# A kernel of two attention and two expert layers on one core: token rows for the first experts scattered to their slots during the first attention

## The reference, cut to what matters

```python
x = x + _L0_xattn_ref(_layernorm(x), ctx_512, ...)   # 16 heads of 8 over a context of 120 x 64
x = x + _L0_ffn_ref(_layernorm(x), Wr, br, W1, b1, W2, b2)   # 8 experts, each token goes to one
x = x + _L1_xattn_ref(_layernorm(x), ctx_512, ...)   # two attentions of 16 heads of 32, each with an MLP
x = x + _L1_ffn_ref(_layernorm(x), router_w, w1, w2) # 64 experts, top 4, capacity 128
```

## Time and profile before

| | us |
|---|---|
| median of three executions (2687.29 to 2694.06) | 2693.37 |
| the profiled execution | 2692.71 |
| its span, first to last instruction | 2691.0 |
| first attention, to the last scatter of token numbers | about 578 |
| first experts, to the last scatter of result rows | about 578 to 789 |
| second attention | about 789 to 2430 |
| second experts and final sum | about 2430 to 2691 |

### The profile page before, as it was taken

The page is one execution under the profiler, slowest core; times in us unless marked ns, Lnnn a source line. Parts: engine busy times, 40 slices in busy tenths (PEclk is TensorE's granted clock), DMA queues, the critical chain, the costliest instruction groups (busy, mean ns, idle before and its releaser), DMA issues. The chain is left out here.

```text
span 2691.0 us, 91904 instructions
## 1 busy us (share of the span) xinstructions
PE 2365.1 (88%) x33576; PEld 1821.1 (68%) x33576; DVE 2012.4 (75%) x6291; ACT 1605.7 (60%) x3346; POOL 1558.9 (58%) x2518
## 2 busy tenths in 40 slices
PE   6888888858768999999999999999999999975766
PEld 5666666647666777777777777777777777753544
DVE  4788888866454788888888888888888888754449
ACT  4556555624434777777777777777777777751110
POOL 1223333337753566666766676676667666646767
PEclk9999999979888999999999999999999999975555
DMA  6223111112110011100000000000000000001128
GB/s 138 65 65 104 50 41 43 42 29 52 42 36 5 7 40 40 38 8 9 9 6 9 8 8 6 8 8 8 7 8 9 8 6 8 5 5 32 48 89 264
DMA packets 129310, 95.31 MB, mean 35 GB/s; under 512 B 42367, under 2 KB 111697, under 8 KB 128482
## 3 DMA queue, kind: packets, MB, share of 16 engines
q1 hardware_dynamic: 109922, 72.53, 9.9%
q0 software_dynamic: 18944, 16.91, 2.4%
HBM read 51.59 MB, written 39.03 MB: 34 GB/s over the span
## 5 line engine op out<-in xcount | busy, mean ns | idle before, releaser
L1227 POOL DMA_INDIRECT list_d<-pay,dest x256 | 268.4, 1048 | 150.0 <-DVE dest L1328 79.6
L1128 POOL TENSOR_SCALAR st_h<-st_h 128x1 f32<-128x1 f32 x192 | 43.8, 228 | 505.0 <-DVE st_h L1334 496.9
L1663 DVE TENSOR_REDUCE rdx<-core 128x16 f32<-128x1920 f32 (+1 forms) x128 | 282.9, 2210 | 54.9 <-PE core L771 54.9
L1071 ACT ACTIVATE kbd<-core 128x1024 f32<-128x1024 f32 (+1 forms) x256 | 245.9, 1012 | 12.2 <-PE core L809 12.2
L804 PE MATMUL core<-qT,pTm 32*128 32x128 f32 (+1 forms) x4096 | 220.7, 285 | 0.4 <-ACT rdx L1057 0.4
L809 PE MATMUL core<-rdx,cst 32*128 32x128 f32 (+1 forms) x4096 | 207.9, 273 | 0.0
L771 PEld LDWEIGHTS core<-pTm,qT 32*128 32x128 f32 x4096 | 125.8, 186 | 98.2 <-issue 95.2
L804 PEld LDWEIGHTS core<-qT,pTm 32*128 32x128 f32 (+1 forms) x4096 | 162.4, 185 | 19.0 <-issue 10.5
L1088 ACT ACT_TABLE_LOAD x128 | 164.2, 1283 | 2.3
L809 PEld LDWEIGHTS core<-rdx,cst 32*128 32x128 f32 (+1 forms) x4096 | 163.6, 186 | 0.0
L1066 ACT ACT_TABLE_LOAD x124 | 159.1, 1283 | 2.2
(11 more groups left out here) (240 smaller groups left out, 7021.6 us busy)
## 6 DMA issues: line engine op xcount, KB each, us to landing
c_d<-zeros SPq DMA_DIRECT2D x64, 256.0 KB
big<-c_d SPq DMA_DIRECT2D x64, 256.0 KB, 3.5
xn_d<-xnS SPq DMA_DIRECT2D x128, 64.0 KB
big<-in_w SPq DMA_DIRECT2D x3, 2048.0 KB, 8.9
yb<-y_d SPq DMA_DIRECT2D x64, 64.0 KB, 1.9
list_d<-pay,dest POOLq DMA_INDIRECT x256, 2.2
out<-big SPq DMA_DIRECT2D x64, 64.0 KB
big<-in_w1T SPq DMA_DIRECT2D x4, 512.0 KB, 4.8
```

The costliest lines, as they stand in the source:

```text
L1071: af(pTb[0:u.T, 2 * k:2 * k + 2, :], core[0:u.T, 2 * k:2 * k + 2, :], ACT.Exp, scale=SCALE).then_inc(s_pexp, 1)
L1227: g_.indirect_dma_start(out=list1_d, out_offset=bass.IndirectOffsetOnAxis(ap=dest[:, v.bs, k:k + 1], axis=0), in_=pay[:, v.bs, k, :], in_o ...
L1663: v_.tensor_reduce(nm[:, :].rearrange("p (g k) -> p g k", g=NG)[:, :, 0:4], core[:, :, 0:4 * T].rearrange("p g (c t) -> p g c t", c=4), AX ...
```

## The change

Three things are changed. POOL scatters the normalised rows themselves to their slots in a new table `xs_d`, right behind the token numbers, in the first attention. The rows therefore come from four buffers `xnR` (in a free part of `big`) instead of two, and SP's stores to `xn0_d` go away. In the first experts SP loads a tile's rows from `xs_d` with a plain transfer, behind the tile's token numbers, and POOL only scatters results. Each expert's region is 128 slots longer, and before it loads the first tile SP writes 128 rows of zeros behind the last filled slot of each expert (1152 rows for the last expert, which also has the empty tiles), at addresses that DVE computes into `filled_i`.

```diff
-    SLOTS0 = E0 * NTOK + TILES0 * P
+    REGION0 = NTOK + P
+    SLOTS0 = E0 * REGION0 + TILES0 * P
-    xn0_d = nc.dram_tensor("xn0_d", (NTOK + P, P), F32).ap()
+    xs_d = nc.dram_tensor("xs_d", (SLOTS0, P), F32).ap()
+        xnR = big[:, 8704:8704 + 4 * P].rearrange("p (u d) -> p u d", d=P)
@@ SP, first attention @@
-                sp.dma_start(xn0_d[NTOK:NTOK + P, :], zeros[:, :]).then_inc(s_init, 16)
-                if at(-3):
-                    store_xn(at(-3), xn0_d)
                 if u:
                     sp.dma_start(c_rows[u.batch], zeros4).then_inc(s_c0, 16)
@@ SP, between the stages and in the first experts @@
+            sp.wait_ge(s_filled, 1)
+            for e in range(E0):
+                at = sp.value_load(filled_i[0:1, e:e + 1], min_val=0, max_val=E0 * REGION0)
+                n = 9 if e == E0 - 1 else 1
+                sp.dma_start(xs_d[bass.ds(at, n * P), :].rearrange("(p a) d -> p a d", a=n),
+                             zeros[:, :].unsqueeze(1).to_broadcast([P, n, P])).then_inc(s_pad, 16)
             for s in range(2):
-                sp.wait_ge(s_sc[s], 16 * (NB // 2))
+                sp.wait_ge(s_sc[s], 32 * (NB // 2))
             sp.wait_ge(s_map, 1)
+            sp.wait_ge(s_pad, 16 * E0)
...
                 sp.dma_start(ids[:, j:j + 1], list0_d[bass.ds(at, P), :]).then_inc(s_ids[k], 16)
+                if positive(n := j + 1 - RING):
+                    sp.wait_ge(s_gt, n)
+                    sp.nop(nofuse=True)
+                sp.dma_start(xg[:, k, :], xs_d[bass.ds(at, P), :]).then_inc(s_ids[k], 16)
@@ POOL, first attention @@
                         ap=dest[:, t5.bs, 0:1], axis=0), in_=tokid[:, t5.bs:t5.bs + 1],
                         in_offset=None).then_inc(s_sc[t5.bs], 16)
+                    g_.indirect_dma_start(out=xs_d, out_offset=bass.IndirectOffsetOnAxis(
+                        ap=dest[:, t5.bs, 0:1], axis=0), in_=xnR[:, t5.batch % 4, :],
+                        in_offset=None).then_inc(s_sc[t5.bs], 16)
@@ POOL, first experts @@
-            for s in range(2):
-                pool.wait_ge(s_xnd[s], 16 * (NB // 2))
-            pool.wait_ge(s_c0, 16 * (CROWS // (4 * P)))
-            experts(TILES0, 0, 6, xn0_d, y0_d, tile_rows, tile_rows, ids_there)
+            for j in range(TILES0):
+                if j == NB // 2 + 4:
+                    context_roots()
+                ids_there(j)
+                scatter(Unit(0, 0, RING, j), j % RING, y0_d, tile_rows(j))
@@ DVE, first attention @@
-                    if positive(n := t3.pair(16)):
-                        dve.wait_ge(s_xnd[t3.bs], n)
-                    normalise(xnS[:, t3.bs, :], xres[:, t3.batch, :], st_n).then_inc(s_xn, 1)
+                    if positive(n := t3.pair(32) - 32):
+                        dve.wait_ge(s_sc[t3.bs], n)
+                    normalise(xnR[:, t3.batch % 4, :], xres[:, t3.batch, :], st_n).then_inc(s_xn, 1)
@@ DVE, after the first attention @@
+            v_.tensor_tensor(filled_i[:, :], count0[0:1, :], cst[0:1, 224:232], ALU.add).then_inc(s_filled, 1)
```

More of the change, by code:

```diff
@@ L203, in build_program @@
         base_i = sb("base_i", [1, TILES0], I32)
+        filled_i = sb("filled_i", [1, E0], I32)
         kT2 = pTm
@@ L285, in build_program @@
         s_sc1 = [sem("s_sc1_even"), sem("s_sc1_odd")]
-        s_map = sem("s_map")
+        s_map, s_filled, s_pad = sem("s_map"), sem("s_filled"), sem("s_pad")
         s_wS = sem("s_wS")
@@ L302, in build_program @@
         s_yld = [sem(f"s_yld{k}") for k in range(RING)]
-        s_cld, CLD = s_ids, 16 * (TILES0 // RING)
+        s_cld, CLD = s_ids, 32 * (TILES0 // RING)
         s_pot, s_poT = sem("s_pot"), sem("s_poT")
@@ L310, in build_program @@
         FIRST = min(8, NB // 2)
-        NINIT = -(-(SLOTS0 // P) // P) + 2
+        NINIT = -(-(SLOTS0 // P) // P) + 1
         class Work:
@@ L570, in _ @@
             for s in range(2):
-                sp.wait_ge(s_xnd[s], 16 * NB)
+                sp.wait_ge(s_xnd[s], 16 * (NB // 2))
         @block.tensor
@@ L667, in half_a @@
                     pe.wait_ge(s_xn, t3.n(1, 1))
-                    tr(m0[:, 256:384], xnS[:, t3.bs, :], ident).then_inc(s_xnt, 1)
+                    tr(m0[:, 256:384], xnR[:, t3.batch % 4, :], ident).then_inc(s_xnt, 1)
                 if t4:
@@ L707, in tokens_in @@
                 k, i = u.r % RING, u.i + u.r // RING
-                pe.wait_ge(s_g[k], u.base * 2 + i * 16 + 16)
+                if u.base:
+                    pe.wait_ge(s_g[k], i * 16 + 16)
+                else:
+                    pe.wait_ge(s_ids[k], i * 32 + 32)
                 if positive(n := u.count(1, -1)):
@@ L1191, in experts @@
                 for j in range(n + lag):
-                    if base == 0 and j == NB // 2 + 4:
-                        context_roots()
                     if j < n:
@@ L1198, in experts @@
                         scatter(Unit(base, 0, RING, j - lag), (j - lag) % RING, dst, to_rows(j - lag))
-            for s in range(2):
-                pool.wait_ge(s_xnd[s], 16 * (NB // 2))
-            pool.wait_ge(s_c0, 16 * (CROWS // (4 * P)))
             def ids_there(j):
-                pool.wait_ge(s_ids[j % RING], j // RING * 16 + 16)
+                pool.wait_ge(s_ids[j % RING], j // RING * 32 + 32)
             tile_rows = lambda j: ids[:, j:j + 1]
-            experts(TILES0, 0, 6, xn0_d, y0_d, tile_rows, tile_rows, ids_there)
+            for j in range(TILES0):
[3 more added lines that the diff above has]
+                scatter(Unit(0, 0, RING, j), j % RING, y0_d, tile_rows(j))
             def mask_pair(u, k):
@@ L1291, in _ @@
             for s in range(2):
-                pool.wait_ge(s_xnd[s], 16 * NB)
+                pool.wait_ge(s_xnd[s], 16 * (NB // 2))
             pool.wait_ge(s_c0, 16 * (CROWS // (4 * P)))
@@ L1383, in dest_a @@
                 after()
-                if positive(n := v.pair(16)):
+                if positive(n := v.pair(32)):
                     dve.wait_ge(s_sc[s], n)
@@ L1482, in _ @@
             after()
-            v_.tensor_scalar(stile[:, :], etile[:, :], float(NTOK), None, ALU.mult)
+            v_.tensor_scalar(stile[:, :], etile[:, :], float(REGION0), None, ALU.mult)
             after()
@@ L1708, in half_b @@
                     dve.wait_ge(s_nrstd, t3.gb(1, 1))
-                    dve.wait_ge(s_xnd[t3.bs], t3.pair(16) + 16 * (NB // 2))
+                    if positive(n := t3.pair(16)):
+                        dve.wait_ge(s_xnd[t3.bs], n)
                     normalise(xnS[:, t3.bs, :], xres[:, t3.batch, :], st_n).then_inc(s_xn, 1)
@@ L1812, in constants @@
     c[:, 160:224] = np.arange(E1)
-    c[:, 224:232] = np.arange(E0) * ntok
+    c[:, 224:232] = np.arange(E0) * (ntok + P)
     c[:, 232:236] = (p[:, None] // D0) % 4 == np.arange(4)
```

7 lines of the change are left out of this document (3 added, 4 removed).

## The result

| | before | changed | ratio, 95% interval |
|---|---|---|---|
| median, us | 2692.76 (2687.29 to 2697.06) | 2677.69 (2672.22 to 2679.76) | 0.9942 (0.9926 to 0.9957) |
| the profiled execution, us | 2692.71 | 2678.57 | |
| its span, us | 2691.0 | 2676.8 | |
| first attention, to the last scatter of token numbers | 576.9 | 596.0 | |
| from there to the last scatter of result rows | 210.8 | 179.3 | |

The changed kernel is 0.6% faster, 15 us where 31 were forecast; the time lies in the stated range of 2645 to 2686, but outside the forecast's own 2655 to 2670. The first experts gained 31.5 us, as forecast (33.0). The first attention lost 19.1 us where 2 were forecast. The rest moved by 1.8 us, which is within what single profiles differ by (see run 12).

A forecast was written before the change was run, and what follows sets the result against it. POOL was taken to bound the first experts, PE and DVE together the first attention. 2692.7 - 33.0 (first experts) + 2 (first attention's burst, net) = 2661.7, say 2662 us; forecast 2655 to 2670, stated range 2645 to 2686.

The forecast's parts named there:

- own sign of being wrong: Wrong if last scatter gains under 25 us from the stage's start, or first attention changes by more than 12 us.
- POOL bounded the first experts: First experts: POOL's 2.59 us a tile gives way to DVE's 2.29 (tiles 0 to 31), then PE's 1.90.
- Roots: First experts: DVE waits 6.6 us for context roots, PE idles 3 to 4, lower clock adds 1.4; together 8.0 us.
- Start of the stage: Start of first experts: writes of zero rows delay the first transpose by 3.9 us; bounds -3 and +8.
- Sum of the stage: First experts: last scatter of results moves from 787.73 to 754.7 us, -33.0 us.
- The burst, net of what the paced loads had cost: First attention: unpaced zeros and weights cost +10 and +3 us, less 10.9 given back; net +2 us.
- My refund of 10.9 us: First attention: five rounds took 51.9 us instead of 41.0 beside paced loads; these 10.9 us come back.
- +10 on the weights and +3 on the zeros: First attention's burst: weights and the writes between them cost 10 us; the other 43 us, zeros alone, cost 3.
- The root may slip 0.1 to 0.2 us of 0.75. I count nothing: First attention: POOL's second scatter delays the root for normalised rows, within its slack before DVE's use; 0 us.
- The bound I gave: First attention: if DVE came directly to POOL's delayed root, the cost would be up to 0.2 x 64 = 13 us.
- DVE's new wait: First attention: DVE waits for a scatter four rounds (33 us) old, long done; no cost counted.
- the one at 2677: First experts: DVE sets the pace of all 72 tiles, late ones also 2.29 us, 15 us more; chance 0.13.

The follow-up runs named there:

- run 12: The kernel before the change, profiled again unchanged; 2683.55 us (one), first attention ending at 572.5 us.
- Experiment 2: Changed kernel with the context roots ahead of POOL's scatter of tile 32 instead of 36; 2671.83 us, ratio 0.9928.
- second profiles: Repeat profiles of both kernels, nothing edited: changed kernel (run 10) 2673.06 us, kernel before (run 12) 2683.55 us.
- run 10: The changed kernel again, unedited, on the same chip as a repeat with the row scatter behind the root; 2673.06 us, ratio 0.9947.
- experiment 6: Changed kernel with the 64 writes of zeros moved from the first to the second attention, one per round; 2659.82 us, ratio 0.9903.
- run 5: Changed kernel with POOL's scatter of rows issued behind the root for the normalised rows instead of ahead; 2666.02 us, ratio 0.9921.

## Why the prediction was right, and where it was not

The time fell into the stated range, but the sum behind it holds one stage that was right and one that was not. By the prediction's own sign of being wrong, a first attention more than 12 us longer, its account of that stage failed: 19.1 us in the first pair of profiles, 16.0 in the second (588.6 against 572.5). That the total still lay in the range is owed to the range's width, which took in rivals up to 2686.

- **POOL bounded the first experts; its gathers gone, two other paces appear.** Right: 2.29 and 1.90 us.
- **Roots.** A wait of 6.6 forecast, 6.85 measured, PE's half clock behind it as forecast. PE stood still for 6.56 us, not the 3 to 4 named. (The forecast's terms, 2.1 + 11.1, give 13.2 and not 13.4, a wait of 6.4.) Experiment 2 takes both away, 8.4 us against the 8.0 of the sum.
- **Start of the stage.** +3.9 forecast, +3.4 measured; the first transpose came 15.4 us after the last list scatter, just short of the 16 to 19 named. (The forecast's terms add to 592.95, not 592.8.) Sum of the stage: -33.0 against -31.5 (-28.3 in the second profiles, 210.1 to 181.8).
- **The burst, net of what the paced loads had cost.** +2 forecast. The first window lost 5 DVE instructions, 1.5 us, against the first profile of before, but 20, 6 us, against the second, whose paced loads cost less; the two second profiles differ by 16, 4.7 us. My refund of 10.9 us was read from one profile and was too large as a mean. Instruction loads behind the queue were seen again. From 69.5 to 80.5 us the changed kernel's queue list (packets, MB, share) has no row for PE's instructions (queue q8):

```profile
q1 hardware_dynamic: 2371, 0.80, 69.1%
q14 instruction: 2, 0.02, 2.2%
```

  and soon after, PE stopped on "issue", for 0.98 us until 83.05 in the first profile and for longer in the second (run 10's timeline):

```profile
85.63 1.97 PE L619 MATMUL core<-pTm,qT 32*128 32x240 f32 x7 [4.00 <-issue]
```

  In calm stretches such a packet comes about every 8 us (12 of them from 166 to 266 us), so a window of 11 us without one says little by itself; but run 10's list has none from 70 to 83 us, and PE stood until 85.63. By the rule in the Trainium skill, DMA: Bandwidth & Descriptors, section Queues, rings and completion order, that each DMA engine takes turns between its queues packet by packet, the burst would cost nothing; experiment 6, which gains 10 us by taking the zeros away, speaks against that result. Inside the term I was wrong on who does it: I put +10 on the weights and +3 on the zeros; the weights alone cost nothing.
- **The step that failed: "The root may slip 0.1 to 0.2 us of 0.75. I count nothing".** The slip was right, and regular rounds hide it. But put behind the root, the same scatter makes the kernel 7.5 us faster side by side, so its place ahead of the root, counted as nothing, costs that much beside the burst. The bound I gave, "if DVE came to it directly, it would be up to 0.2 x 64 = 13 us", is not exceeded, but the path is another: no regular round grew. The time goes in disturbed rounds, in which PE stops on "issue" and runs at the lower clock level behind it: 5.4 us of such waits and 1294 instructions in the second window of the changed kernel, none and 1345 in run 5. How POOL's order would make these stops longer or more frequent, no run shows: the stop at 533 us begins before POOL's root is late. That the slack of POOL and DVE catches up after a stop is not seen either: in the kernel before, after intervals of 13.3, 10.0, 9.6 and 11.0 us between list scatters, from 118 us on, come 8.1 and 8.4 again and none shorter. Nor does the place cost anything by itself: run 6, with the scatter ahead of the root and no burst, counts 1338 there, as many as the kernel before. So the 7.5 us are shown; what links POOL's order to PE's stops, the root's lost slack or only the moment at which the scatter goes out, stays open.
- **DVE's new wait "is long done".** True: the wait ahead of `xnR`, for a scatter four rounds old, never held DVE. What did, once, is a wait that the prediction doesn't name. It stands ahead of the token numbers (line 1401), for the scatters of two rounds ago, and now counts the scatter of rows too: nothing in the rounds of 8 us, 2.79 us in the drain, where list scatters are 3 to 6 us apart.

The parts of the first profile: -31.5 + 1.5 + 13.2 + 2.8 + 1.6 (unassigned) - 1.8 (behind the first experts) = -14.2, the 14.1 between the profiled executions. Of these, 13.2 and 1.5 are one pair of profiles' values: between the second profiles the two windows differ by 28 and 16 instructions, 8.2 and 4.7 us. Of the rivals, the one at 2677 has the right time by the wrong reason: late tiles take 1.90 us, not 2.29.

## What to carry to other kernels

That a trace shows an added instruction hidden in the regular rounds doesn't yet price it: here its place on POOL cost 7.5 us beside a burst of transfers and nothing that showed without it. Where the order is free, put new work behind the instruction that others wait for, and time both orders side by side. Bulk writes with a late deadline belong in the stage with the emptiest queues, one per round, not where the loads already are: moving the zeros gained some 10 us, pacing them in place gained nothing sure. And compare progress in fixed windows by the instruction count of an engine with a fixed list, over two profiles of each kernel, before a term is read from one episode.

## What the runs showed of the hardware

- The same kernel's first attention ended at 596.0 and 588.6 us in two profiles, and that of the kernel before at 576.9 and 572.5: a few disturbed rounds more or less. A whole execution varies by as much (2672 to 2680).
- A DVE instruction took longer beside the issue of a POOL scatter. In run 5 the scatter of rows mostly falls on DVE's normalisation; the groups of DVE's instructions, 160 to 560 us, in that run:

```profile
L1353 DVE TENSOR_SCALAR big<-xres,st_n 128x128 f32<-128x128 f32 x49 | 23.7, 485 | 0.0
```

  The same instruction took 346 ns in the changed kernel, where the scatter came earlier, and in run 5 itself it took 0.53 us at 315.26, inside a scatter's 1.06 us, and 0.34 at 307.20, at a scatter's end. It was hidden: no regular round grew.
